# First attention's output turned by transposing SBUF transfers, its projection later in the step

## The chip, the cores and the metric

The kernel runs on one core of one Trainium2 chip. The metric is device time in microseconds of one execution. The engines of the core named here are PE (TensorE, the matrix engine; PEld is its loading of weights), DVE (VectorE), ACT (ScalarE), POOL (GpSimd) and SP (SyncE, which issues transfers here and computes nothing). Each works through its own list of instructions in order; semaphores tie the lists together.

## The reference, cut to what matters

One post-norm decoder layer over 16 sequences of 256 tokens with 256 features: first attention (16 heads of 64, causal), second attention over 77 context rows with a mask, and a mixture of 8 experts (two per token). A normalisation follows each part.

```python
q, k, v = (einsum('bxy,iyk->bxik', x, W).reshape(h, b, t, hs) for W in (Wq, Wk, Wv))
wei = softmax(where(causal, einsum('hbqd,hbkd->hbqk', q, k) * hs ** -0.5, -inf))
out = einsum('hbqk,hbkd->hbqd', wei, v).reshape(b, t, h * hs)
x = layernorm(x + out @ proj_w.T + proj_b)
x = layernorm(x + second_attention(x, ctx, mask))
x = layernorm(x + experts(x))
```

The change concerns the line with `proj_w`: what comes out of first attention has positions on the partitions, and the projection needs it with the features of a head there.

## The kernel before

The program has four parts in a row: both attentions (until about 1010 us), routing, the experts, and a last normalisation. The change is in the first.

The attention part works on 32 tiles of 128 tokens. A step `s` holds work on several tiles at once: q, k and v of tiles `s+1` and `s+2` (`fill`, six pieces a tile, with high and low f16 halves made by ACT, `hi`, and DVE, `lo`), first attention of tile `s` (eight groups: `scores`, DVE's `maxima`, ACT's `exps`, `turn_probs` on PE, high and low halves `pt` by ACT and DVE, `pv` on PE; after each odd group DVE's `normalise`), projection, first norm and most of second attention of tile `s-1` (`stage_c`, pieces 0 to 7), and its end for tile `s-2` (`pv2`, `stage_d`). Nothing is scheduled at run time: in each engine's block a function `step(s)` writes these calls in an order chosen by hand, and the engine runs them in that order. SP's `step` does so for the transfers, all through one queue.

The path that is changed: `normalise` writes the normalised output of two groups into `o_norm`; ACT copies its high half into `o_st` (`o_high`), POOL subtracts for the low half (`split_o`), counted by `s_o_lo`, four a tile. In `stage_c(t, 0)` PE turns `o_st` of the tile by 16 transposes into two PSUM banks, and ACT and DVE each copy one bank into `o_t`. In `stage_c(t, 1)` PE multiplies `o_t` with the projection's weights (32 matmuls into bank c5; in every other step the key and value products of second attention come first), DVE adds the bias to y1, takes statistics (`stats_of`, `moments`), POOL makes the inverse deviation, and DVE's `first_norm` writes x1. `stage_c(t, 2)` begins with PE's transposes of x1. Since `o_norm` has one place, `normalise` waits until POOL has read the pair before.

## Time and profile before

| | us |
|---|---|
| median of 3 runs (lowest, highest) | 1508.05 (1507.47, 1509.12) |
| the profiled execution | 1509.21 |
| its span, first to last instruction | 1507.5 |
| PE busy | 1301.3 (86%) |
| DVE busy | 1083.8 (72%) |
| ACT busy | 924.1 (61%) |
| POOL busy | 721.1 (48%) |
| first and last turn of `o_st` on PE (512 in 32 steps) | 77.9 and 981.5, so 29.1 a step |

A row's busy share is an average over parts with different limits: the attention steps take some 900 of the 1507.5 us, and only there the change does something. Waits are read from a timeline: a row is a run of like instructions, with its start, its time, and in brackets how long the engine had been idle before it and who ended that. Times of PE rows overlap by some 0.15 us, since matmuls are pipelined; the time that a piece takes from PE is that from its start to the next one's.

### The profile page before, as it was taken

To read this page: it belongs to the slowest core of one execution; us is meant where nothing else is said; L and a number is where in the kernel's file an instruction comes from. 1 tells how busy PE (TensorE), PEld (TensorE's weight loads), DVE (VectorE), ACT (ScalarE), POOL (GpSimd) and SP (SyncE) were. 2 spreads that over 40 slices of the span, in tenths; PEclk is the share of its full clock that TensorE was granted. 3 is DMA by queue.
4 is the path that set the end of the run, shared out by engine and by line. 5 is a ranking of instruction groups with operands and counts; after the bars stand their busy time and mean duration, and the time that the engine had idled before them with its cause. 6 is when DMAs were issued, how large, how long until landed. Compare 5 with 4: busy or idle time off the path is not lost. (4 is left out here: it accounts for less than half of the span.)

```text
span 1507.5 us, 47409 instructions
## 1 busy us (share of the span) xinstructions
PE 1301.3 (86%) x16821; PEld 1079.2 (72%) x16821; DVE 1083.8 (72%) x3112; ACT 924.1 (61%) x2287; POOL 721.1 (48%) x970
## 2 busy tenths in 40 slices
PE   3589999999999999999999999864899999999930
PEld 2478778778878877887887887632688888888820
DVE  4678888888888888888888888748455555555537
ACT  3566777778777777777877766514344444444426
POOL 3144564674565566566556644420243344343326
PEclk9899999999999999999999999995899999999975
DMA  9657767667657667676676664019333363333235
GB/s 222 145 138 161 171 169 160 137 145 175 142 140 184 132 140 190 130 150 155 154 154 142 153 105 90 24 61 421 125 75 76 75 163 93 80 75 77 70 139 206
DMA packets 293216, 208.95 MB, mean 139 GB/s; under 512 B 218782, under 2 KB 250654, under 8 KB 290560
## 3 DMA queue, kind: packets, MB, share of 16 engines
q1 hardware_dynamic: 281952, 184.01, 51.0%
q0 software_dynamic: 6816, 17.71, 4.1%
q10 hardware_dynamic: 4224, 4.19, 0.8%
q8 instruction: 146, 2.39, 0.7%
q14 instruction: 78, 0.64, 0.1%
HBM read 93.79 MB, written 65.93 MB: 106 GB/s over the span
## 5 line engine op out<-in xcount | busy, mean ns | idle before, releaser
L1729 PE MATMUL ps_e<-xt,wres 128*128 128x128 f16 x3408 | 343.5, 220 | 5.2 <-DMA xt<-xg 4.2
L1729 PEld LDWEIGHTS ps_e<-xt,wres 128*128 x3408 | 285.8, 99 | 77.1 <-issue 5.9
L1793 ACT ACTIVATE act_g<-ps_e,b 128x128 f32<-128x128 f32 x568 | 162.4, 369 | 208.1 <-PE ps_e L1729 206.3
L1736 PE MATMUL ps_e<-wres,g_hi 128*128 x568 | 214.5, 379 | 0.8 <-DVE g_lo L1816 0.8
L743 ACT ACTIVATE probs<-st_k,nmax 128x128 f32<-128x128 f32 (+1 forms) x512 | 199.9, 448 | 1.9 <-DVE nmax L964 1.6
L964 DVE CUSTOM_DVE_ANT_0 st_k<-ps,causal 128x128 f32<-128x128 f32 (+1 forms) x512 | 160.6, 351 | 38.0 <-PE ps L444 37.9
L1696 POOL DMA_INDIRECT z_scr<-e_y,dst_i x71 | 82.9, 1168 | 212.6 <-DVE e_y L1807 212.6
L750 ACT ACTIVATE pt_hi<-ps 128x384 f16<-128x384 f32 x256 | 125.2, 489 | 56.0 <-PE ps L452 27.7
L1738 PE MATMUL ps_e<-wres,g_lo 128*128 x568 | 154.8, 273 | 0.0
L452 PE MATMUL ps<-ident,probs 128*128 128x128 f32 x768 | 130.5, 279 | 24.4 <-ACT probs L743 19.3
L969 DVE TENSOR_TENSOR pt_lo<-ps,pt_hi 128x384 f16<-128x384 f32 x256 | 141.4, 552 | 6.0 <-ACT pt_hi L750 2.6
L1804 DVE SCALAR_TENSOR_TENSOR e_y<-ps_e,b 128x256 f32<-128x256 f32 x71 | 30.1, 425 | 158.9 <-PE ps_e L1738 158.9
L1271 POOL TENSOR_TENSOR o_st<-o_norm,o_st 128x256 f16<-128x256 f32 x128 | 86.4, 675 | 104.5 <-ACT o_st L758 104.5
L506 PE MATMUL ps<-proj_pair,o_t 128*128 128x256 f16 x1024 | 117.7, 273 | 3.1 <-DVE o_t L1014 3.0
L452 PEld LDWEIGHTS ps<-ident,probs 128*128 128x128 f32 x768 | 86.4, 141 | 45.8 <-ACT probs L743 33.5
L506 PEld LDWEIGHTS ps<-proj_pair,o_t 128*128 128x128 f16 x1024 | 112.2, 146 | 7.2 <-ACT o_t L782 6.8
L1304 POOL TENSOR_TENSOR var_eps<-mv,eps 128x1 f32<-128x1 f32 x64 | 12.3, 192 | 203.1 <-DVE mv L989 203.0
L1392 POOL DMA_INDIRECT xg<-pair_scr,tok_i x71 | 69.7, 982 | 71.7 <-DVE tok_i L1619 42.8
L470 PE MATMUL ps<-v_pos,pt_hi 128*128 128x65 f16 x768 | 90.6, 193 | 13.3 <-DVE o_norm L979 11.2
L422 PE MATMUL ps<-x_hi,w_k 128*128 128x128 f16 x1024 | 97.3, 220 | 0.1
L422 PE MATMUL ps<-x_hi,w_q 128*128 128x128 f16 x1024 | 96.8, 220 | 0.2 <-DVE v_tok L942 0.2
L470 PEld LDWEIGHTS ps<-v_pos,pt_hi 128*128 128x128 f16 x768 | 73.8, 99 | 26.4 <-issue 22.8
(281 smaller groups left out, 4044.9 us busy)
## 6 DMA issues: line engine op xcount, KB each, us to landing
k_pair<-k_pair SPq DMA_DIRECT2D x96, 256.0 KB, 6.6
st_p<-in_moe_w SPq DMA_DIRECT2D x24, 768.0 KB, 5.8
w_scr<-st_p SPq DMA_DIRECT2D x24, 768.0 KB, 4.1
wres<-w_scr SPq DMA_DIRECT2D x18, 1024.0 KB, 20.9
v_scr<-v_tok SPq DMA_DIRECT2D x32, 512.0 KB, 4.2
v_pos<-v_scr SPq DMA_DIRECT2D x64, 256.0 KB, 6.1
q_st<-st_q SPq DMA_DIRECT2D x64, 128.0 KB, 2.8
z_scr<-zero SPq DMA_DIRECT2D x32, 256.0 KB, 3.3
```

Of the source, the lines that this page charges most:

```text
L422: last = mm(bank[:, i * P:(i + 1) * P], w[:, b, c, 4 * n + i].rearrange("p k d -> p (k d)"), xs[a][:, c], start=(m == 0), stop=(m == 5))
L452: last = nc.tensor.transpose(ps_t[:, b * P:(b + 1) * P], probs[:, g % 2, b * P:(b + 1) * P], ident[:])
L470: last = mm(ps_o[:, at:at + 1 + HS], a[:, g % 2, blk * P:(blk + 1) * P], v[:, 0:1 + HS], start=(m == 0), stop=(m == len(todo) - 1), skip_g ...
L506: last = mm(c5[:, 0:D], o_t[:, :, h], wp[:, k, h], start=(h == 0 and k == 0), stop=(h == H - 1 and k == 1))
L743: nc.scalar.activation(probs[:, g % 2, lo_:up_], masked[:, g % 2, lo_:up_], ACT.Exp, bias=nmax[:, g % 2, q:q + 1], scale=-1.0).then_inc(s_ ...
L750: nc.scalar.activation(pt_hi[:, g % 2], ps_t[:, 0:384], ACT.Copy).then_inc(s_pt_hi, 1)
L964: nc.vector.tensor_tensor_reduce(masked[:, g % 2, lo_:up_], ps_s[:, lo_:up_], causal[:].rearrange("p n k -> p (n k)")[:, lo_:up_], -SCORE_ ...
L969: nc.vector.tensor_tensor(pt_lo[:, g % 2], ps_t[:, 0:384], pt_hi[:, g % 2], ALU.subtract).then_inc(s_pt_lo, 1)
L1729: last = mm(out, w(c * FF + f * P, b, P), xt[:, t % X_BUFS, a, c], start=(m == 0), stop=(m == 5))
L1736: mm(out[:, 0:2 * D], g_hi[:, t % G_BUFS, f], w(KC * FF + f * D, 0, 2 * D), start=(f == 0), stop=False, skip_group_check=True)
L1738: last = mm(out[:, 0:D], g_lo[:, t % G_BUFS, f], w(KC * FF + f * D, 0, D), start=False, stop=(f == FC - 1), skip_group_check=True)
L1793: nc.scalar.activation(act_g[:, k % 2, f], ps[:, 3 + 2 * (k % 2) + f // 4, (f % 4) * P:(f % 4 + 1) * P], ACT.Gelu, bias=bias[:, f:f + 1], ...
```

## The change

`o_st` is no longer turned by PE. SP issues transposing transfers from `o_st` to `o_t`, both in SBUF: two for the pairs of groups 1 and 3 together, two for group 5 and two for group 7 (one for each half of the partitions), at the three places of SP's `step` that the diff shows. With that `stage_c(t, 0)` and the two copies into `o_t` are gone, `o_t` has another layout, and the projection reads it so. On PE the projection (`stage_c(s-1, 1)`) is written after `turn_probs(s, 1)` instead of after `scores(s, 3)`; ACT and DVE have their parts of it correspondingly later, and DVE has `lo(s+1, 4)` and the statistics of the second norm ahead of `first_norm`. `o_norm` has two places, so that `normalise` waits for the pair before last. Left out below are the list of semaphores and POOL's two index changes.

```diff
@@ -138,9 +138,9 @@
     rden = sb("rden", [P, 4], F32)
     pt_hi = sb("pt_hi", [P, 2, 384], F16)
     pt_lo = sb("pt_lo", [P, 2, 384], F16)
-    o_norm = sb("o_norm", [P, 4, HS], F32)
+    o_norm = sb("o_norm", [P, 2, 4, HS], F32)
     o_st = sb("o_st", [P, 2, 2 * GROUPS, 2, HS], F16)
-    o_t = sb("o_t", [P, P, H], F16)
+    o_t = sb("o_t", [P, 2, 2 * GROUPS, HS], F16)
     x_bias = sb("x_bias", [P, D], F32)
     y1 = sb("y1", [P, D], F32)
     y2 = sb("y2", [P, D], F32)
@@ -320,6 +320,15 @@
             sp.dma_start(q_st[HS:P, p, :, 1], q_low[HS:P]).then_inc(s_qlow, 16)
             sp.wait_ge(s_qmove, 16 * (t + 1))
             sp.dma_start(q_st[HS:P, p, :, 0], q_low[0:HS]).then_inc(s_qlow, 16)
+
+        def turn_output(t, g):
+            p = t % 2
+            sp.wait_ge(s_o_lo, 4 * t + g // 2 + 1)
+            if g == 3 and since(t, 1):
+                sp.wait_ge(s_proj, t)
+            n = slice(0 if g == 3 else 2 * (g - 1), 2 * (g + 1))
+            for a in range(2):
+                sp.dma_start_transpose(o_t[:, a, n], o_st[a * HS:(a + 1) * HS, p, n].rearrange("p n k d -> p (n k d)")).then_inc(s_ot, 16)
 
         def load_rows(t):
             p = t % 2
@@ -360,6 +369,9 @@
                 load_x(s + 2)
             if has(s + 1):
                 v_out(s + 1)
+            if has(s - 1):
+                turn_output(s - 1, 7)
+            if has(s + 1):
                 v_in(s + 1)
                 key_move(s + 1)
                 key_double(s + 1)
@@ -369,14 +381,19 @@
                 load_context(half(s))
             if has(s + 1):
                 query_move(s + 1)
+            if has(s + 1):
                 query_low(s + 1)
             if has(s - 2):
                 x2_out(s - 2)
                 pair_out(s - 2)
+            if has(s):
+                turn_output(s, 3)
             if 0 <= s - 4 < PIECES:
                 piece_out(s - 4)
             if 0 <= s - 3 < PIECES:
                 piece_in(s - 3)
+            if has(s):
+                turn_output(s, 5)
             if 0 <= s < ZERO_STEPS:
                 zeros(s)
 
@@ -477,18 +494,10 @@
         def stage_c(t, g):
             p = t % 2
             busy(t, BUSY_C.get(g, 0))
-            if g == 0:
-                pe.wait_ge(s_o_lo, 4 * (t + 1))
+            if g == 1:
+                pe.wait_ge(s_ot, 96 * (t + 1))
                 if since(t, 1):
                     pe.wait_ge(s_t2_lo, 4 * t)
-                for half_, bank in enumerate((c5, c6)):
-                    b16 = bank.bitcast(F16)
-                    for n in range(8):
-                        last = nc.tensor.transpose(b16[:, n * P:(n + 1) * P].rearrange("p (t a i) -> p a t i", a=2, i=PAIRS), o_st[:, p, 8 * half_ + n].rearrange("p k d -> p (k d)"), ident16[:])
-                    last.then_inc(s_ot, 1)
-            if g == 1:
-                pe.wait_ge(s_ot_a, t + 1)
-                pe.wait_ge(s_ot_d, t + 1)
                 if t == 0:
                     pe.wait_ge(s_lo, splits_until("xo"))
                 if p == 0:
@@ -503,7 +512,7 @@
                     last.then_inc(s_kv2, 1)
                 for h in range(H):
                     for k in range(2):
-                        last = mm(c5[:, 0:D], o_t[:, :, h], wp[:, k, h], start=(h == 0 and k == 0), stop=(h == H - 1 and k == 1))
+                        last = mm(c5[:, 0:D], o_t[:, h // PAIRS].rearrange("p n (t i) -> p i (n t)", i=PAIRS)[:, h % PAIRS], wp[:, k, h], start=(h == 0 and k == 0), stop=(h == H - 1 and k == 1))
                 last.then_inc(s_proj, 1)
             if g == 2:
                 pe.wait_ge(s_x1, t + 1)
@@ -613,29 +622,26 @@
             if has(s):
                 turn_probs(s, 0)
                 scores(s, 2)
-            if has(s - 1):
-                stage_c(s - 1, 0)
             if has(s - 2):
                 pv2(s - 2, 1)
             if has(s):
                 scores(s, 3)
+                pv(s, 0)
+            if has(s - 2):
+                stage_d(s - 2, 1)
+            if has(s):
+                scores(s, 4)
+                turn_probs(s, 1)
             if has(s - 1):
                 stage_c(s - 1, 1)
-            if has(s):
-                pv(s, 0)
+            if has(s + 1):
+                fill(s + 1, 4)
             if has(s - 1):
                 value_rows(s - 1, 0)
             if has(s - 2):
-                stage_d(s - 2, 1)
-            if has(s):
-                scores(s, 4)
-                turn_probs(s, 1)
+                stage_d(s - 2, 2)
             if has(s - 1):
                 value_rows(s - 1, 1)
-            if has(s + 1):
-                fill(s + 1, 4)
-            if has(s - 2):
-                stage_d(s - 2, 2)
             if has(s):
                 turn_probs(s, 2)
             if has(s - 1):
@@ -754,8 +760,8 @@
             pair = 4 * t + g // 2
             act.wait_ge(s_o_norm, pair + 1)
             if g == 1 and since(t, 2):
-                act.wait_ge(s_ot, 2 * (t - 1))
-            nc.scalar.activation(o_st[:, p, 2 * (g - 1):2 * (g + 1), 0], o_norm[:], ACT.Copy).then_inc(s_o_hi, 1)
+                act.wait_ge(s_ot, 96 * (t - 1))
+            nc.scalar.activation(o_st[:, p, 2 * (g - 1):2 * (g + 1), 0], o_norm[:, pair % 2], ACT.Copy).then_inc(s_o_hi, 1)
 
         def exp2(t, cc):
             act.wait_ge(s_shift, 2 * t + cc + 1)
@@ -777,9 +783,6 @@
 
         def stage_c(t, g):
             p = t % 2
-            if g == 0:
-                act.wait_ge(s_ot, 2 * t + 1)
-                nc.scalar.activation(o_t[:, 0:64].rearrange("p t h -> p (t h)"), c5.bitcast(F16), ACT.Copy).then_inc(s_ot_a, 1)
             if g == 1:
                 if p == 0:
                     act.wait_ge(s_kv2, half(t) + 1)
@@ -828,16 +831,10 @@
                     late_split(0)
             if has(s + 1):
                 hi(s + 1, 3)
-            if has(s - 1):
-                stage_c(s - 1, 0)
             if has(s):
                 exps(s, 2)
-            if has(s - 1):
-                stage_c(s - 1, 1)
             if 0 <= s - 4 < PIECES:
                 piece(s - 4)
-            if has(s - 1):
-                value_rows(s - 1, 0)
             if has(s - 2):
                 stage_d(s - 2, 1)
             if has(s):
@@ -845,9 +842,12 @@
                 if s == 0:
                     late_split(1)
             if has(s - 1):
-                value_rows(s - 1, 1)
+                stage_c(s - 1, 1)
             if has(s + 1):
                 hi(s + 1, 4)
+            if has(s - 1):
+                value_rows(s - 1, 0)
+                value_rows(s - 1, 1)
             if has(s - 1):
                 stage_c(s - 1, 2)
             if has(s):
@@ -974,9 +974,9 @@
             dve.wait_ge(s_pv, 2 * pair + 2)
             nc.vector.reciprocal(rden[:], o[:, :, 0]).then_inc(s_rden, 1)
             dve.wait_ge(s_rden, pair + 1)
-            if since(t, 1) or g > 1:
-                dve.wait_ge(s_o_lo, pair)
-            nc.vector.tensor_tensor(o_norm[:], o[:, :, 1:1 + HS],
+            if since(t, 1) or g > 3:
+                dve.wait_ge(s_o_lo, pair - 1)
+            nc.vector.tensor_tensor(o_norm[:, pair % 2], o[:, :, 1:1 + HS],
                                     rden[:].unsqueeze(2).to_broadcast([P, 4, HS]), ALU.mult).then_inc(s_o_norm, 1)
 
 
@@ -1009,9 +1009,6 @@
 
         def stage_c(t, g):
             p = t % 2
-            if g == 0:
-                dve.wait_ge(s_ot, 2 * t + 2)
-                nc.vector.tensor_copy(o_t[:, 64:128].rearrange("p t h -> p (t h)"), c6.bitcast(F16)).then_inc(s_ot_d, 1)
             if g == 1:
                 if p == 0:
                     dve.wait_ge(s_kv2_hi, 2 * (half(t) + 1))
@@ -1079,10 +1076,6 @@
                 pt(s, 0)
                 if s == 0:
                     late_split(0)
-            if has(s - 1):
-                stage_c(s - 1, 1)
-                stats_of(s - 1, 0, y1, s_y1, s_ln1)
-                moments(s - 1, 0, s_ln1, s_mv1)
             if has(s - 2):
                 stage_d(s - 2, 1)
             if has(s):
@@ -1091,15 +1084,18 @@
                 if s == 0:
                     late_split(1)
             if has(s - 1):
-                first_norm(s - 1)
+                stage_c(s - 1, 1)
+                stats_of(s - 1, 0, y1, s_y1, s_ln1)
+                moments(s - 1, 0, s_ln1, s_mv1)
+            if has(s + 1):
+                lo(s + 1, 4)
             if has(s - 2):
                 stage_d(s - 2, 2)
                 stats_of(s - 2, 1, y2, s_y2, s_ln2)
                 moments(s - 2, 1, s_ln2, s_mv2)
             if has(s - 1):
+                first_norm(s - 1)
                 stage_c(s - 1, 2)
-            if has(s + 1):
-                lo(s + 1, 4)
             if has(s - 2):
                 second_norm(s - 2)
             if has(s):
@@ -1162,8 +1158,6 @@
                 stage_c(s - 1, 7)
             if has(s + 1):
                 maxima(s + 1, 2)
-            if has(s):
-                stage_c(s, 0)
             if has(s + 2):
                 lo(s + 2, 3)
             if has(s - 1):
```

PE's list at the place where the step begins, before the change, in a step without key and value products: `scores(s, 3)` (k_pair), the projection (o_t), and the first row of `pv(s, 0)` (v_pos).

```order
L441 MATMUL ps<-k_pair,q_st 128x128 [waits s1_11_max]
L442 MATMUL ps<-k_pair,q_st 128x128
L443 MATMUL ps<-k_pair,q_st 128x256
L444 MATMUL ps<-k_pair,q_st 128x256
L506 MATMUL ps<-proj_pair,o_t 128x256 [waits s1_23_ot_d,s1_22_ot_a]
L506 MATMUL ps<-proj_pair,o_t 128x256 x31
L470 MATMUL ps<-v_pos,pt_hi 128x65 [waits s1_18_o_norm,s1_9_v_in,s1_15_pt_lo]
```

The same place after the change.

```order
L458 MATMUL ps<-k_pair,q_st 128x128 [waits s1_11_max]
L459 MATMUL ps<-k_pair,q_st 128x128
L460 MATMUL ps<-k_pair,q_st 128x256
L461 MATMUL ps<-k_pair,q_st 128x256
L487 MATMUL ps<-v_pos,pt_hi 128x65 [waits s1_18_o_norm,s1_9_v_in,s1_15_pt_lo]
L490 MATMUL ps<-v_pos,pt_hi 128x64
```

The rows of `pv(s, 0)`, which wait for DVE's low halves of the probabilities (pt_lo), now follow the scores directly. The projection stands behind the transposes of probabilities of group 1 and before the fill of q, as PE's list after the change shows:

```order
L469 MATMUL ps<-ident,probs 128x128 [waits s1_15_pt_lo,s1_12_exp]
L469 MATMUL ps<-ident,probs 128x128 x2
L515 MATMUL ps<-proj_pair,o_t 128x256 [waits s1_46_t2_lo,s1_21_ot]
L515 MATMUL ps<-proj_pair,o_t 128x256 x31
L439 MATMUL ps<-x_hi,w_q 128x128 [waits s1_7_fill_lo]
```

It waits for `s_ot`, which the transfers now raise.

DVE's list from y1 to the first norm (the row `x<-y,mv,rstd`) before the change:

```order
L1026 SCALAR_TENSOR_TENSOR y<-ps,x_bias 128x256 [waits s1_xb,s1_24_proj]
L985 BN_STATS stats<-y 128x6 [waits s1_25_y1]
L989 BN_AGGR mv<-stats 128x2 [waits s1_26_ln1]
L1059 TENSOR_TENSOR o_lo<-ps,o_hi 128x256 [waits s1_53_o2_hi]
L964 ISA st_k,nmax<-ps,causal 128x128 [waits s1_12_exp,s1_10_scores]
L964 ISA nmax 128x1
L964 ISA st_k,nmax<-ps,causal 128x256
L964 ISA nmax 128x1
L969 TENSOR_TENSOR pt_lo<-ps,pt_hi 128x384 [waits s1_14_pt_hi]
L1008 TENSOR_SCALAR x<-y,mv,rstd 128x256 [waits s1_27_rstd1]
```

And after it:

```order
L969 TENSOR_TENSOR pt_lo<-ps,pt_hi 128x384 [waits s1_14_pt_hi]
L1023 SCALAR_TENSOR_TENSOR y<-ps,x_bias 128x256 [waits s1_xb,s1_22_proj]
L985 BN_STATS stats<-y 128x6 [waits s1_23_y1]
L989 BN_AGGR mv<-stats 128x2 [waits s1_24_ln1]
L950 TENSOR_TENSOR st_q<-ps,q_st 128x128x4 [waits s1_qlow,s1_6_fill_hi]
L1060 SCALAR_TENSOR_TENSOR y<-ps,x 128x256 [waits s1_53_proj2]
L985 BN_STATS stats<-y 128x6 [waits s1_54_y2]
L989 BN_AGGR mv<-stats 128x2 [waits s1_55_ln2]
L1008 TENSOR_SCALAR x<-y,mv,rstd 128x256 [waits s1_25_rstd1]
```

The maxima and pt_lo of group 1 have moved ahead of y1; the low half of q (st_q, which waits for ACT's high half of that fill) and y2 with its statistics now stand between y1's moments and the norm.

SP's list around the end of a step, after the change (before it, the four DMA_TRANSPOSE rows are missing):

```order
L331 DMA_TRANSPOSE o_t<-o_st 128x8x64 [waits s1_22_proj,s1_20_o_lo]
L331 DMA_TRANSPOSE o_t<-o_st 128x8x64
L280 DMA w_scr<-st_p 128x3072 [waits s1_w_lo]
L276 DMA st_p<-in_moe_w 128x1536 [waits s1_w_lo]
L331 DMA_TRANSPOSE o_t<-o_st 128x4x64 [waits s1_20_o_lo]
L331 DMA_TRANSPOSE o_t<-o_st 128x4x64
L257 DMA x_t<-in_xT 128x2x128 [waits s1_4_x_lo]
L289 DMA v_scr<-v_tok 128x2x1024 [waits s1_9_v_in,s1_7_fill_lo,s1_6_fill_hi]
```

The third pair of transposes, for group 7, follows that last row (`v_out`) and stands before `v_in`. So `load_x` and `v_out` are queued behind the transposes of group 5, and `v_in` behind those of group 7.

## Rows read from the trace of the kernel before

**Rows 1.** Busy time by stage: stage, its us, each engine's busy us, PE clock, DMA share, GB/s
```profile
300.00:500.00 200.00, 188.19 (x2630) 163.07 (x2627) 169.58 (x550) 155.14 (x337) 118.77 (x169) 1.00 0.67 155
```

**Rows 2.** PE's timeline, one step from scores(s, 2): start, us, instructions, idle before
```profile
574.88 0.22 PE L441 MATMUL ps<-k_pair,q_st 128*128 128x128 f16 x1
...
575.22 1.06 PE L487 MATMUL ps<-ident,o_st 128*128 128x128 f16 x16
576.11 0.18 PE L577 MATMUL ps<-st_xq,pt_hi 128*128 128x34 f16 x1
...
576.49 0.22 PE L441 MATMUL ps<-k_pair,q_st 128*128 128x128 f16 x1
...
577.15 3.69 PE L506 MATMUL ps<-proj_pair,o_t 128*128 128x256 f16 x32 [0.16 <-DVE o_t L1014]
580.67 0.19 PE L470 MATMUL ps<-v_pos,pt_hi 128*128 128x65 f16 x1
...
581.86 0.22 PE L422 MATMUL ps<-x_hi,w_q 128*128 128x128 f16 x1
...
583.20 0.27 PE L597 MATMUL ps<-xw_o,o_hi 128*128 128x256 f16 x1
...
584.18 0.38 PE L513 MATMUL ps<-ident,x 128*128 128x128 f32 x2
...
587.24 0.49 PE L452 MATMUL ps<-ident,probs 128*128 128x128 f32 x3
```

**Rows 3.** DVE's timeline in the same step
```profile
576.31 0.69 DVE L1014 COPY o_t<-ps 128x1024 f16<-128x1024 f16 x1 [0.25 <-PE ps L487]
576.92 0.68 DVE L953 SCALAR_TENSOR_TENSOR k_pair<-ps,k_pair 128x512 f16<-128x512 f32 x1
...
578.14 0.28 DVE L964 CUSTOM_DVE_ANT_0 st_k<-ps,causal 128x128 f32<-128x128 f32 x1
...
578.69 0.55 DVE L969 TENSOR_TENSOR pt_lo<-ps,pt_hi 128x384 f16<-128x384 f32 x1
580.88 0.42 DVE L1026 SCALAR_TENSOR_TENSOR y<-ps,x_bias 128x256 f32<-128x256 f32 x1 [1.63 <-PE ps L506]
...
581.89 0.39 DVE L1059 TENSOR_TENSOR o_lo<-ps,o_hi 128x256 f16<-128x256 f32 x1
...
583.22 0.41 DVE L1008 TENSOR_SCALAR x<-y,mv,rstd 128x256 f32<-128x256 f32 x1
```

**Rows 4.** PE's timeline in step 0: scores(0, 3) and pv(0, 0)
```profile
51.62 0.23 PE L441 MATMUL ps<-k_pair,q_st 128*128 128x128 f16 x1 [0.74 <-DVE nmax L964]
...
54.28 0.20 PE L470 MATMUL ps<-v_pos,pt_hi 128*128 128x65 f16 x1 [2.16 <-DVE pt_lo L969]
```

**Rows 5.** ACT's timeline in the step of rows 2: the high half of q
```profile
583.39 0.60 ACT L732 ACTIVATE q_st<-ps 128x512 f16<-128x512 f32 x1 [0.85 <-PE ps L422]
```

**Rows 6.** PE's timeline later in that step, and in the next
```profile
600.93 0.77 PE L545 MATMUL ps<-ident,probs 128*128 128x128 f32 x5 [0.70 <-ACT probs L767]
...
623.84 0.19 PE L470 MATMUL ps<-v_pos,pt_hi 128*128 128x65 f16 x1 [0.56 <-DVE o_norm L979]
```

**Rows 7.** The tile xt of the experts: ns min/median/max, first and last start in us
```profile
L1729 PE MATMUL ps_e<-xt,wres x3408: 219/219/314, 1068.1 to 1441.6; 128*128 128x128 f16 x190
L1769 SPq DMA_TRANSPOSE xt<-xg x71: 1189/1190/2646, 1065.2 to 1427.5; - x71
```

**Rows 8.** DMA queues, 1250 to 1400 us: packets, MB, share of 16 engines
```profile
q1 hardware_dynamic: 15776, 3.80, 14.2%
```

**Rows 9.** POOL's (o_st) and SP's timelines around the start of the step of rows 2
```profile
571.77 0.67 POOL L1271 TENSOR_TENSOR o_st<-o_norm,o_st 128x256 f16<-128x256 f32 x1
574.40 0.67 POOL L1271 TENSOR_TENSOR o_st<-o_norm,o_st 128x256 f16<-128x256 f32 x1 [1.96 <-ACT o_st L758]
...
570.18 0.93 SPq L257 DMA_DIRECT2D x_t<-in_xT  x1
573.21 0.38 SPq L289 DMA_DIRECT2D v_scr<-v_tok  x1
```

More of the change, by code:

```diff
@@ L198, in attention_block @@
     (s_xt, s_xn, s_ctx, s_x_hi, s_x_lo, s_fill, s_fill_hi, s_fill_lo, s_v_out, s_v_in, s_scores, s_max,
-     s_exp, s_pt, s_pt_hi, s_pt_lo, s_pv, s_rden, s_o_norm, s_o_hi, s_o_lo, s_ot, s_ot_a, s_ot_d, s_proj, s_y1,
+     s_exp, s_pt, s_pt_hi, s_pt_lo, s_pv, s_rden, s_o_norm, s_o_hi, s_o_lo, s_ot, s_proj, s_y1,
      s_ln1, s_rstd1, s_x1, s_x1t, s_x1_hi, s_x1_lo, s_c_hi, s_c_lo, s_q2, s_q2_hi, s_q2_lo, s_kv2, s_kv2_hi,
@@ L204, in attention_block @@
         "xt xn ctx x_hi x_lo fill fill_hi fill_lo v_out v_in scores max exp pt pt_hi pt_lo pv rden o_norm o_hi "
-        "o_lo ot ot_a ot_d proj y1 ln1 rstd1 x1 x1t x1_hi x1_lo c_hi c_lo q2 q2_hi q2_lo kv2 kv2_hi kv2_lo bd s2 "
+        "o_lo ot proj y1 ln1 rstd1 x1 x1t x1_hi x1_lo c_hi c_lo q2 q2_hi q2_lo kv2 kv2_hi kv2_lo bd s2 "
         "pred mx2 shift exp2 t2 t2_hi t2_lo pv2 rden2 o2n o2t o2_hi o2_lo proj2 y2 ln2 rstd2 x2 x2_hi x2_lo "
@@ L633, in step @@
             if has(s - 1):
-                value_rows(s - 1, 1)
+                stage_c(s - 1, 1)
             if has(s + 1):
                 fill(s + 1, 4)
+            if has(s - 1):
+                value_rows(s - 1, 0)
             if has(s - 2):
                 stage_d(s - 2, 2)
+            if has(s - 1):
+                value_rows(s - 1, 1)
             if has(s):
@@ L830, in step @@
                 hi(s + 1, 3)
-            if has(s - 1):
-                stage_c(s - 1, 0)
             if has(s):
                 exps(s, 2)
-            if has(s - 1):
-                stage_c(s - 1, 1)
             if 0 <= s - 4 < PIECES:
                 piece(s - 4)
-            if has(s - 1):
-                value_rows(s - 1, 0)
             if has(s - 2):
@@ L847, in step @@
             if has(s - 1):
-                value_rows(s - 1, 1)
+                stage_c(s - 1, 1)
             if has(s + 1):
                 hi(s + 1, 4)
+            if has(s - 1):
+                value_rows(s - 1, 0)
+                value_rows(s - 1, 1)
             if has(s - 1):
@@ L1081, in step @@
                     late_split(0)
-            if has(s - 1):
-                stage_c(s - 1, 1)
-                stats_of(s - 1, 0, y1, s_y1, s_ln1)
-                moments(s - 1, 0, s_ln1, s_mv1)
             if has(s - 2):
@@ L1093, in step @@
             if has(s - 1):
-                first_norm(s - 1)
+                stage_c(s - 1, 1)
+                stats_of(s - 1, 0, y1, s_y1, s_ln1)
+                moments(s - 1, 0, s_ln1, s_mv1)
+            if has(s + 1):
+                lo(s + 1, 4)
             if has(s - 2):
@@ L1270, in split_o @@
             pool.wait_ge(s_o_hi, pair + 1)
-            nc.gpsimd.tensor_tensor(at[:, :, 1], o_norm[:], at[:, :, 0], ALU.subtract).then_inc(s_o_lo, 1)
+            nc.gpsimd.tensor_tensor(at[:, :, 1], o_norm[:, pair % 2], at[:, :, 0], ALU.subtract).then_inc(s_o_lo, 1)
         def split_x2(t):
```

## Prediction

> **What bounds the kernel now.** I read the table of stages first: where the attention steps run (300 to 500 us), PE is busy 188.19 of 200 us at a granted clock of 1.00, DVE 169.58, ACT 155.14, and the DMA engines 0.67 [rows 1]. PE is the bound, with about 6% idle: with the table's 29.1 us a step that is 29.1 x 11.81/200 = 1.7 us of waits a step. DVE comes close behind and, since every engine runs its list in order, what decides is not the sum of PE's work but which of its waits are covered. So I read PE's timeline through one step, from `scores(s, 2)` at 574.88 on [rows 2], and beside it DVE's for the same stretch [rows 3]. The reader should see two things. PE has almost no holes: 16 transposes, the rest of second attention's value product, scores, then 32 projection matmuls from 577.15 to 580.67. And DVE, at 578.14, is only then doing the maxima of `scores(s, 3)` and at 578.69 the low halves of the probabilities of group 0, which PE's `pv(s, 0)` waits for. PE comes to `pv(s, 0)` at 580.67, when they have been ready since 578.69 + 0.55 = 579.24. The projection is what PE does meanwhile; DVE then has nothing to do for 1.63 us until the projection lands [rows 3].
>
> **What is removed.** Per step: the 16 transposes, 576.11 - 575.22 = 0.89 us of PE; the hole before the projection, of which 0.16 us is a wait for DVE's copy and which is 0.33 us in all (577.15 - 576.49 = 0.66, less 0.33 for the four score matmuls, 574.88 to 575.22) [rows 2]. On DVE the copy (0.69 us), on ACT its twin. If nothing else changed PE would gain 0.89 + 0.33 = 1.22 us a step.
>
> **What is moved: the first wait.** In the new order PE goes from `scores(s, 2)` through pv2 (0.38) and `scores(s, 3)` (0.33) straight to `pv(s, 0)`, which it reaches 0.34 + 0.38 + 0.33 = 1.05 us after 574.88, at 575.93, if nothing holds it. DVE's order before that probability block is unchanged but for the copy: maxima 2 (done at 576.31 - 0.25 = 576.06, the copy's row says that DVE was idle 0.25 us before it), then the low half of k, the reciprocal and the normalised second output (576.92 to 578.14, 1.22 us), maxima 3 (0.55), pt_lo (0.55): 576.06 + 2.32 = 578.38 [rows 3], 578.44 with a handover. PE thus waits 578.44 - 575.93 = 2.5 us, part of it before `scores(s, 3)` (which needs maxima 2), most before `pv(s, 0)`. The trace of before shows this very order once: step 0 has no projection to put there, and PE waited 0.74 us before `scores(0, 3)` and 2.16 us before `pv(0, 0)`, 2.9 us together [rows 4]. Bounds: 2.0 (if half the DVE chain were done earlier) and 2.9; I take 2.5.
>
> **The second wait.** The projection itself keeps its 3.52 us (577.15 to 580.67). What lies between `pv(s, 0)` and it costs 581.86 - 580.67 = 1.19 as before, so it starts at 578.44 + 1.19 = 579.63 and ends at 583.15. Behind it, PE now has only the fill (581.86 to 583.20, 1.34) and the output product of second attention with a turn of probabilities (583.20 to 584.18, 0.98) before it transposes x1: it wants x1 at 585.47. DVE's way to x1: y1 starts 0.21 after PE has moved on, its sum, statistics and moments take 581.89 - 580.88 = 1.01. But three things now stand ahead of the norm on DVE: `lo(s+1, 4)`, which must wait for that fill and ACT's high half (ACT ends 583.39 + 0.60 = 583.99 where PE's fill ended 583.20, so 0.79 later [rows 5]: 584.49 + 0.79 = 585.28), takes about 0.7; then y2 with its statistics, another 1.01; then the norm, 0.41 [rows 3]. 585.28 + 0.06 for the handover + 0.7 + 1.01 + 0.41 = 587.5. PE waits 2.0 us for x1, where before x1 was there at 583.22 + 0.41 = 583.63 and PE came at 584.18. POOL's two small operations fall into DVE's wait. Bounds: 0 if DVE's list were not in order, 2.1.
>
> From x1's transposes to the turn of group 3 nothing changes (584.18 to 587.24, 3.06), so that turn stands at 587.5 + 3.06 = 590.56: 3.32 us later in the step than before (2.5 + 2.0 - 1.2, less rounding).
>
> **What is given back.** After that point PE's old waits can absorb some. Two are shown: 0.70 us before second attention's transposes (for ACT's exponentials, behind a long POOL chain) and, in every other step, 0.56 us before a pv, for a normalised output that stood behind POOL's subtraction [rows 6]. The second goes away with two places of `o_norm`. The first is at the end of a chain that starts at the shifted softmax scores, which are themselves about 3 us late; I count 0.27 back (bounds 0 and 0.70). Two steps: 2 x 3.32 - 0.27 - 0.56 = 5.8 us. Steps 1 to 31 hold 15.5 such pairs: **+90 us**. All of PE's idle, 1.7 us a step, would be the most that could be absorbed: 31 x (3.32 - 1.7) = +50 us, the lower bound.
>
> **The transposing transfers.** The trace has 71 of the kind, 128 x 512 f16 (128 KB) each: 1.19 us of SP's queue (slowest 2.65), first issue at 1065.2 and first matmul on its result at 1068.1, so landed within 2.9 us [rows 7]. In a stretch with 29 of them queue 1 held 16 engines 14.2% of 150 us, 0.73 us each [rows 8]. A step moves 512 KB in six issues, so 4 x 0.73 = 2.9 us of the engines in 32: no new bound beside 0.67. When is the last pair there? POOL ends pair 2 at 571.77 + 0.67 = 572.44. SP then issues two transposes (0.6 each by bytes, 1.19 by instruction), `load_x` (0.93), `v_out` (0.38), then the last two, whose data POOL had at 575.07 [rows 9]: the second of these is issued at 575.7 to 577.4 and lands by 578.6 to 580.3. PE wants it at 579.63. Late by 0 to 0.7; I take 0.25, nearer the issue by bytes: 31 x 0.25 = **+8 us**. With the slowest issue of the trace each time (2.65) it would be 5 us late. The other queued transfers (v, k and q moves) shift by 2 to 3 us with `v_out`; their readers stand near the end of the step. The drained last step pays a transfer's latency where 0.89 us of transposes and a copy stood: +1 us.
>
> The row says 0.73 us of engine time for four blocks of 128 x 128. The Trainium skill (VectorE: DVE Perf Modes, "The three transpose paths") gives 1309 ns for one such block by DMA against 390 ns by TensorE, and advises TensorE when PSUM will do. By its figure taken block by block, an estimate, the last four blocks would take 5.2 us in place of 2.9, some 2 us later a step; I keep the row.
>
> **Sum.** 1509.21 us, the profiled execution (span 1507.5), + 90 + 8 + 1 = 1608. The median of the runs shown is 1.2 us below that execution: **1607 us**, slower by 6.5%.
>
> **Rivals.**
> - *Late transposes.* Issue cost goes by instruction, or halves of 64 partitions cost more than 128, and PE waits for o_t 2 us or more a step. For it: six issues stand in one in-order queue with transfers that wait for each other. Against: rows 7 and 8. 1599 + 31 x 2 = 1661, from 1645 up.
> - *Mostly absorbed.* PE's own 1.7 us of waits vanish, since DVE and ACT have 0.69 and 1.0 us less to do: 1508 + 50 + up to 8 = 1558 to 1566. Against: the waits listed are tails of chains that the projection starts.
> - *Faster.* PE is the bound and sheds 1.22 us a step: 1508 - 31 x 1.22 = 1470. It decides if DVE has pt_lo of group 0 within 0.7 us of `scores(s, 2)` and x1 within 2.3 us of the projection; the rows give 3.2 and 4.35. It would need DVE to be ahead of PE, and DVE waits for PE there (maxima 2 start 0.2 us after the scores).
> - *No change.* The two cancel by chance.
>
> **Numbers.** Forecast (1575 to 1645) 0.64, late transposes 0.13, absorbed (1530 to 1575) 0.13, faster 0.07, no change 0.03. The range 1553 to 1662 holds the forecast, most of the absorbed and half of the late case, 0.8. About 0.2% is what a measurement of this kernel tells from no change: slower 0.90, same 0.03, faster 0.07.
>
> **What will show it.** In the changed trace: PE waits near 2 us before the first `pv` of each step, released by DVE's pt_lo, and near 2 us before the x1 transposes, released by DVE's norm; a pair of steps takes 58 + 6 us; the row of o_t transposes shows how SP pays, and PE's wait before the projection whether they land in time. If the first two waits are under 1 us the forecast is wrong; if the wait before the projection is the largest, the second case holds.

## The result and the profile after

The changed kernel takes **1751.91 us** (median of 4 runs, 1748.35 to 1756.93) against 1508.05 of the kernel before: ratio 1.162, 95% interval 1.158 to 1.165. It is slower, as forecast, but by 244 us and not by 99; the range ended at 1662. Of the rivals the late transposes came closest, and they too were priced too low (1661). By the prediction's own sign that case holds: of PE's waits between 200 and 900 us the one for the transfers is the largest (56.4 us, against 42.8 before `scores(s, 3)` and `pv(s, 0)` and 25.6 for x1).

The table of stages of the changed kernel, same columns and stretch as [rows 1]:

```profile
300.00:500.00 200.00, 157.17 (x1999) 129.25 (x1996) 135.25 (x440) 120.31 (x270) 98.38 (x137) 0.92 0.63 133
```

PE is busy 157 of 200 us, not 188, and its granted clock is 0.92 where it was 1.00. The second number is the one nobody had asked for. The first projection starts at 92.1, the last at 1233.0: 36.8 us a step against 29.1, so 7.7 us more. Where they go, PE's timeline of one step shows (start, us, what, idle before and who ended it; to be held against [rows 2]):

```profile
571.61 0.22 PE L458 MATMUL ps<-k_pair,q_st 128*128 128x128 f16 x1
...
572.84 0.23 PE L458 MATMUL ps<-k_pair,q_st 128*128 128x128 f16 x1 [0.37 <-DVE nmax L964]
...
575.21 0.20 PE L487 MATMUL ps<-v_pos,pt_hi 128*128 128x65 f16 x1 [1.87 <-DVE pt_lo L969]
...
576.08 0.49 PE L469 MATMUL ps<-ident,probs 128*128 128x128 f32 x3
579.83 5.75 PE L515 MATMUL ps<-proj_pair,o_t 128*128 128x256 f16 x32 [3.26 <-DMA o_t<-o_st]
585.42 0.22 PE L439 MATMUL ps<-x_hi,w_q 128*128 128x128 f16 x1
...
589.64 0.44 PE L522 MATMUL ps<-ident,x 128*128 128x128 f32 x2 [1.74 <-DVE x L1008]
```

Both forecast waits are there: 0.37 + 1.87 us around `scores(s, 3)` and `pv(s, 0)` (forecast 2.5) and 1.74 us before the x1 transposes (forecast 2.0). Two things are not as forecast. The projection waits 3.26 us for the transposing transfers (forecast 0.25), and it then lasts from 579.83 to 585.42, 5.59 us in place of 3.52, which the forecast had left alone. The table of stages, cut along that stretch, says why; the last three columns are PE's granted clock, the DMA share and GB/s:

```profile
575.21:576.57 1.36, 1.36 (x18) 1.10 (x18) 0.00 (x0) 0.00 (x0) 0.00 (x0) 1.00 1.02 343
576.57:579.83 3.26, 0.00 (x0) 0.00 (x1) 0.00 (x0) 3.00 (x3) 0.00 (x0) 0.61 0.88 251
579.83:582.00 2.17, 2.17 (x11) 1.70 (x12) 1.44 (x6) 0.62 (x2) 0.00 (x0) 0.50 0.65 107
582.00:585.42 3.42, 3.42 (x24) 2.94 (x23) 0.00 (x0) 0.00 (x0) 0.00 (x0) 0.69 1.41 117
585.42:587.90 2.48, 2.48 (x35) 2.19 (x32) 1.35 (x4) 0.60 (x1) 0.76 (x2) 1.00 0.80 174
```

The clock fell to half (0.50: 1.2 in place of 2.4 GHz) while PE stood idle, and the projection began at that level: 11 matmuls in 2.17 us. The next stretch has 0.69 in the mean; in it the clock came back to 1.00, at about 584.1, when 4.2 us of the projection were over. Over the whole run the projection's group shows it too; before, the mean of one matmul was 273 ns and the sum 117.7 us, and `pv` had waited 13.3 us in all where its line now has 61.9:

```profile
L515 PE MATMUL ps<-proj_pair,o_t 128*128 128x256 f16 x1024 | 165.1, 338 | 54.7 <-DMA o_t<-o_st 54.7
L487 PE MATMUL ps<-v_pos,pt_hi 128*128 128x65 f16 x768 | 91.8, 194 | 61.9 <-DVE pt_lo L969 60.5
```

Why the transfers are late is read on POOL's and SP's own timelines of that step; the first two rows are POOL's low halves for groups 5 and 7, the rest is SP's queue, where a row's time is what the issues occupy SP (before: [rows 9]):

```profile
568.50 0.67 POOL L1265 TENSOR_TENSOR o_st<-o_norm,o_st 128x256 f16<-128x256 f32 x1
571.12 0.67 POOL L1265 TENSOR_TENSOR o_st<-o_norm,o_st 128x256 f16<-128x256 f32 x1 [1.96 <-ACT o_st L764]
...
566.70 2.55 SPq L331 DMA_TRANSPOSE o_t<-o_st  x2
569.29 1.54 SPq L280 DMA_DIRECT2D w_scr<-st_p  x1
570.88 0.43 SPq L276 DMA_DIRECT2D st_p<-in_moe_w  x1
571.36 3.16 SPq L331 DMA_TRANSPOSE o_t<-o_st  x2
574.57 0.59 SPq L257 DMA_DIRECT2D x_t<-in_xT  x1
575.26 0.43 SPq L289 DMA_DIRECT2D v_scr<-v_tok  x1
575.74 2.60 SPq L331 DMA_TRANSPOSE o_t<-o_st  x2
```

From 566.70 to 578.34 SP has no pause. Group 5's data are ready at 569.17 and are issued from 571.36 on; group 7's are ready at 571.79 and issued from 575.74 on. A pair costs 2.55 us where its halves are 128 KB (the pairs of groups 1 and 3) and 2.60 where they are 64 KB (group 7): SP pays by instruction. The row of the tile `o_t` gives the same over 192 issues (ns, lowest, median, highest), with the time that PE lost before the projection (L515) or, in the steps with key and value products, before those (L508), and how long a transfer took to land:

```profile
L331 SPq DMA_TRANSPOSE o_t<-o_st x192: 1170/1266/2811, 74.3 to 1224.3; - x192
...
  PE ps L515: 54.7, 15
...
  PE ps L508: 35.6, 14
...
DMA to landing us min/median/max: 2.3/3.7/7.4
```

So PE lost 54.7 + 35.6 = 90.3 us to the transfers in the whole run.

### The profile page after: what moved, and what is told of

It is laid out like the page before. It is cut to its first block and busy times, and to the rows that moved or that the text cites. A ratio compares the mean times of both kernels' runs of the same rounds, so it can differ in the third digit from the quotient of the medians.

```text
span 1755.1 us, 46505 instructions
## 1 busy us (share of the span) xinstructions
PE 1351.8 (77%) x16306; PEld 1087.7 (62%) x16306; DVE 1074.4 (61%) x3080; ACT 895.2 (51%) x2255; POOL 724.2 (41%) x970
## 3 DMA queue, kind: packets, MB, share of 16 engines
q10 hardware_dynamic: 4224, 4.19, 0.7%
## 5 line engine op out<-in xcount | busy, mean ns | idle before, releaser
L515 PE MATMUL ps<-proj_pair,o_t 128*128 128x256 f16 x1024 | 165.1, 338 | 54.7 <-DMA o_t<-o_st 54.7
L515 PEld LDWEIGHTS ps<-proj_pair,o_t 128*128 128x128 f16 x1024 | 139.4, 154 | 80.7 <-DMA o_t<-o_st 58.9
L469 PE MATMUL ps<-ident,probs 128*128 128x128 f32 x768 | 135.3, 286 | 28.3 <-ACT probs L749 23.7
L738 ACT ACTIVATE q_st<-ps 128x512 f16<-128x512 f32 x64 | 38.2, 597 | 203.6 <-PE ps L439 203.6
L487 PE MATMUL ps<-v_pos,pt_hi 128*128 128x65 f16 x768 | 91.8, 194 | 61.9 <-DVE pt_lo L969 60.5
L1284 POOL TENSOR_TENSOR k_bd<-head_rows,k 128x308 f16<-128x308 f16 x64 | 45.3, 728 | 169.5 <-DVE v L1019 169.5
L1386 POOL DMA_INDIRECT xg<-pair_scr,tok_i x71 | 69.6, 980 | 73.5 <-DVE tok_i L1613 42.8
## 6 DMA issues: line engine op xcount, KB each, us to landing
wres<-w_scr SPq DMA_DIRECT2D x18, 1024.0 KB, 23.2
```

The costliest lines, as they stand in the source:

```text
L469: last = nc.tensor.transpose(ps_t[:, b * P:(b + 1) * P], probs[:, g % 2, b * P:(b + 1) * P], ident[:])
L487: last = mm(ps_o[:, at:at + 1 + HS], a[:, g % 2, blk * P:(blk + 1) * P], v[:, 0:1 + HS], start=(m == 0), stop=(m == len(todo) - 1), skip_g ...
L515: last = mm(c5[:, 0:D], o_t[:, h // PAIRS].rearrange("p n (t i) -> p i (n t)", i=PAIRS)[:, h % PAIRS], wp[:, k, h], start=(h == 0 and k == ...
```

## Experiments

Three theories of the missing 145 us. **A, the order**: the waits for DVE are larger than forecast, or others joined them. **B, SP's queue**: the transfers are late because of where they stand among SP's issues. **C, the clock**: PE runs slower behind its new waits. All times are medians; each set was timed beside the kernel before (1508.2 to 1508.5).

### The order alone

```diff
             if g == 1:
-                pe.wait_ge(s_ot, 96 * (t + 1))
+                pe.wait_ge(s_ot_a, t + 1)
+                pe.wait_ge(s_ot_d, t + 1)
...
                 scores(s, 2)
+            if has(s - 1):
+                stage_c(s - 1, 0)
```

> The changed kernel's order on every engine and its two places for the normalised output, but the kernel before's turning: 16 TensorE transposes a step and the two copies out of PSUM, no transposing transfer. The order alone. By the forecast the order costs 90 us net of the transposes and the hole that went, 1.22 us x 32 = 39 us; with the transposes back, 0.89 x 32 = 28: 1508 + 90 + 28 = 1626, range 1600 to 1650. If the lower clock behind the new waits comes with the order and not with the transfers, 1650 to 1690. If the order is harmless and the transfers are all of the loss: 1500 to 1540.

Measured 1661.05, ratio 1.101 (1.098 to 1.104). The order costs 153 us without any transfer, 35 more than the 118 that the waits of the forecast give (1508 + 90 + 28 = 1626). Its waits between 200 and 900 us (total, times, longest):

```profile
PE ps L472 <- DVE pt_lo L969: 48.7, 21, 2.3
PE ps L515 <- DVE x L1008: 26.5, 20, 1.7
```

They are 2.3 and 1.3 us a step, no more than forecast. The wait for x1 is 1.74 and 0.91 us in turn: the larger one, near the forecast 2.0, in the steps without key and value products, the kind that the forecast read, the smaller one in the others. But the clock is 0.96 between 300 and 500 us here, and a projection matmul takes 296 ns. In one step PE stood for 2.32 us, until 322.81, waiting for pt_lo, and from 323 to 326 us, in which the projection began, the granted clock was 0.50.

### The order alone, PE kept working

```diff
                 scores(s, 3)
+                idle_work(s, 8)
                 pv(s, 0)
```

`idle_work` are matmuls of 512 columns on constants, into a bank that is written anew before it is read.

> The run of the order alone (TensorE transposes and copies, the changed order) with 8 matmuls of 512 columns, on operands that are there and into a bank that nobody reads, ahead of pv(s,0), where TensorE waits 2.3 us a step for pt_lo. The order alone measured 1661 where the waits of the forecast give 1626. If the 35 us are the lower clock behind that wait, the time falls by 25 to 40, to 1620 to 1636. If they are other waits: 1655 to 1670.

Measured **1620.18**, 41 us less, with more work on PE. The wait for pt_lo is down to 12.5 us, the other is as it was, and the clock is 1.00 again:

```profile
300.00:500.00 200.00, 177.57 (x2357) 147.31 (x2355) 153.11 (x490) 136.18 (x302) 107.70 (x152) 1.00 0.60 135
...
PE ps L521 <- DVE x L1015: 27.4, 21, 1.7
...
PE ps L478 <- DVE pt_lo L976: 12.5, 21, 0.6
```

C holds for the order: 41 us of its 153 go with the clock. What is left, 112, is the 118 of the forecast within 6: A is ruled out as the miss, though the 6 come of two errors that nearly cancel (below).

### The changed kernel, PE kept working

```diff
                 scores(s, 3)
+                idle_work(s, 8)
                 pv(s, 0)
...
+                idle_work(s, 11)
                 stage_c(s - 1, 1)
```

> The changed kernel with matmuls put into two of its waits, on operands that are there and into a bank that nobody reads: 8 of 512 columns ahead of pv(s,0), 11 ahead of the projection (some 0.22 us each at full clock, 1.8 and 2.4 us, less than the two waits of 1.9 and 3.3 us). They change nothing but what TensorE does while it waits. If the lower clock after these waits costs time by itself (theory: the projection takes 5.6 us in place of 3.5 because the clock is at half in it), the projection comes back to about 3.5 us and the time falls by 45 to 65 us, to 1687 to 1707. If the clock is low for another reason, or the time that the projection loses is waited for elsewhere anyway, 1740 to 1765. If the matmuls stand before work that is ready: up to 1780.

Measured 1718.91, 33 us less than the changed kernel: in the direction of C, and less than its 45 to 65. PE's clock is 0.99 between 300 and 500 us, and the projection's group is down from 165.1 to 128.4 us, 37 us, about what the kernel gained:

```profile
L521 PE MATMUL ps<-proj_pair,o_t 128*128 128x256 f16 x1024 | 128.4, 288 | 29.7 <-DMA o_t<-o_st 29.7
```

At 288 ns a matmul, not 273, the projection is not wholly at the upper level; PE still waits for the transfers behind the 11 matmuls, 29.7 us before the projection alone.

### Without the last pair of transfers

```diff
-            if has(s - 1):
-                turn_output(s - 1, 7)
...
-                pe.wait_ge(s_ot, 96 * (t + 1))
+                pe.wait_ge(s_ot, 64 * (t + 1))
...
+        nc.vector.memset(o_t[:, :, 12:16], 0.0).then_inc(s_one, 1)
```

> The changed kernel without group 7's transposing transfers: the last quarter of the turned output is a constant zero, so a quarter of the projection's input is left out. The transfers of groups 3 and 5 have landed long before the projection. If the transfers' lateness is what was sized wrongly and the rest stands as forecast (order and waits for DVE: about +90 us over the kernel before), the wait for the turned output goes to 0 and the time to 1590 to 1650, the lower half if the clock stays up too. If the order itself was sized wrongly: 1680 or more with no wait for the turned output left.

Measured 1643.02: 109 us are tied to group 7's pair. PE's wait for transfers is down to 6.7 us in the whole run, from 90.3. The clock is still low (0.93 between 300 and 500 us, with the wait for pt_lo as it was), which fits a time at the upper end.

### The six transfers in a row, ahead of the weight piece

```diff
             if has(s):
                 turn_output(s, 3)
+                turn_output(s, 5)
+                turn_output(s, 7)
             if 0 <= s - 4 < PIECES:
                 piece_out(s - 4)
```

> The changed kernel with the same six transposing transfers, in one row on SP's queue: group 7's directly behind group 5's, in the same step, ahead of the piece of the expert weights, the load of x and v_out (SP alone is reordered, and ScalarE's two weight pieces go behind pt(s,1), since their load now comes later). If the transfers are late because of where they stand on SP, where each instruction takes about 1.27 us, group 7's pair begins near 572 in place of 575.74 in the step that was read, the projection's wait falls from 3.3 to under 1 us, and the time falls by 70 to 100 us, to 1650 to 1680, some 45 more if the clock then stays up (1605 to 1635). If the transfers are late because they take so long in the DMA engines: 1735 to 1760. If the loads that now stand behind them become the wait: over 1700 with new DMA rows on TensorE or ScalarE.

Measured 1750.57: nothing gained. Read by its time alone this would refuse B. Its waits between 200 and 900 us say otherwise:

```profile
PE ps L520 <- DVE x L1006: 47.3, 18, 5.1
...
PE ps L568 <- DVE v L1017: 19.2, 9, 2.8
PE ps L456 <- issue: 13.0, 12, 6.2
...
PE ps L513 <- DMA o_t<-o_st: 0.2, 1, 0.2
```

The wait for the transfers is gone (0.2 us), and a wait for x1 of up to 5.1 us stands in its place, with two others. The cause of the first is on ACT's timeline:

```profile
571.42 1.48 ACT L821 ACTIVATE st_p<-st_p 128x1536 f16<-128x1536 f32 x1 [3.94 <-DMA st_p<-in_moe_w]
572.93 1.48 ACT L823 ACTIVATE st_p<-st_p 128x1536 f32<-128x1536 f32 x1
574.32 0.58 ACT L736 ACTIVATE q_st<-ps 128x512 f16<-128x512 f32 x1
```

The load of the weight piece now stands behind six transposes. ACT waits 3.94 us for it, and q's high half is queued behind; DVE's `lo(s+1, 4)`, y2 and the norm wait for that half. The run was confounded by its own edit, and the next one mends it.

### The six transfers in a row, behind the weight piece

```diff
                 piece_in(s - 3)
             if has(s):
+                turn_output(s, 3)
                 turn_output(s, 5)
+                turn_output(s, 7)
```

> The changed kernel with the six transposing transfers in one row on SP's queue, as in the run that put group 7 behind group 5, but behind the piece of the expert weights, not ahead of it, and ScalarE's order as in the changed kernel: the weight piece that ScalarE waits for is then issued some 3 us earlier than in the changed kernel, and no new wait is made. Group 7's pair begins when the other four are through, about 573.2 to 573.5 in the step that was read, 2.3 to 2.5 us earlier than 575.74. If the place on SP is what makes the turned output late, the projection's wait falls from 3.3 to about 1 us a step, the time by 60 to 80 us and some 20 to 40 more if the clock stays up: 1640 to 1690. If the reordering moves the loss to another wait again, as it did with the weight piece: 1730 to 1755.

Measured **1650.86** (1646.57 and 1655.15): 101 us less by the order of SP's list alone, the same six transfers and the same bytes, which take as long from issue to landing (median 3.6 us, 3.7 in the changed kernel). PE's wait for the transfers is 8.1 us in the whole run (from 90.3), 7.7 of it before the projection:

```profile
  PE ps L513: 7.7, 8
```

B holds. With its place on SP mended the change is 10 us under the order alone (1661), where 0.25 us of lateness and 0.89 us of saved transposes had promised 8 - 28 = -20. The traces show where the rest went. From the fifth projection on (232.92 to 1125.78 us, against 222.19 to 1135.96) the kernel is 21 us faster than the order alone; until then it is 11 us slower. In the first steps PE waits 5.25, 4.83 and 4.19 us before `scores` with no releaser named; this wait is 23.2 us in the whole run and was 10.3 in the changed kernel. SP's list has the writes of zeros in the first four steps as well; which transfer is late there was not tested.

### Both at once

```diff
                 scores(s, 3)
+                idle_work(s, 8)
                 pv(s, 0)
```

on the kernel of the section before.

> The run with the six transposing transfers in a row behind the weight piece (1651), with the 8 matmuls on unread data ahead of pv(s,0) that took 41 us off the order alone. If the two things that the forecast of 1607 left out are SP's place for the transfers and the clock behind TensorE's wait for pt_lo, and nothing else, this kernel gives about the forecast: 1651 - 41 = 1610, range 1595 to 1625. If the two overlap, or a third loss is there: 1635 or more.

Measured 1629.10, 22 us less and not 41, 4 us above the expected range and 22 above the forecast of 1607. The clock is 1.00; PE is earlier, and the transfers, which keep their time, are late again by about 0.5 us a step, 14.9 us in all with 2.0 before the key and value products:

```profile
  PE ps L519: 12.9, 14
```

So the two losses overlap in part: this wait is 7 us more than in the run before and than forecast. The first steps are the other part of what is left over the forecast: the fifth projection starts at 227.97, where the order alone with PE kept working has 216.06, 12 us earlier. 7 + 12 is about the 22. This is read from the traces and was not tested; the gain of 22 in place of 41 is accounted for in part only, by the 7.

### The second wait undone

```diff
                 moments(s - 1, 0, s_ln1, s_mv1)
+                first_norm(s - 1)
             if has(s + 1):
                 lo(s + 1, 4)
...
-                first_norm(s - 1)
                 stage_c(s - 1, 2)
```

on the order alone with PE kept working (1620).

> The order alone with the 8 matmuls ahead of pv(s,0) (1620), with VectorE's first_norm put directly behind the moments of y1, ahead of lo(s+1,4) and the statistics of y2: the second wait of the forecast undone. If x1 is late because of what VectorE does ahead of it, it can come at POOL's 1/deviation, 0.9 to 1.5 us earlier a step; TensorE's wait for x (1.3 us a step) falls under 0.5, the time by 25 to 40 us, to 1580 to 1595. If the wait for x is that chain itself, whatever stands in it, or lo(s+1,4) and y2 are then late in its place: 1610 to 1625.

Measured 1603.07, 17 us less, between the two ranges. The wait for x1 is gone (2.6 us between 200 and 900 us, from 27.4), and with a wait of 1.3 us a step it should have given 40 us. Part of it has come back in waits that were smaller (L553: 10.4 us) or not there:

```profile
PE ps L553 <- ACT probs L775: 15.8, 22, 0.7
...
PE ps L545 <- DVE q_lo L1041: 4.9, 22, 0.3
PE ps L521 <- ACT st_xv L784: 3.6, 11, 0.3
...
PE ps L521 <- DVE x L1015: 2.6, 11, 0.2
```

So what DVE does ahead of the norm is what made x1 late, as forecast, but taking that away gives back less than half of what it costs: this wait lost 25 us between 200 and 900 us, and the first three rows have gained 14. Why those grew was not tested.

### Transposing transfers in the order of before

Two mixtures were meant as faster kernels. They keep the order of before and two places of `o_norm`. In the first SP turns groups 1, 3 and 5, PE the last 4 blocks; in the second SP turns groups 1 and 3, PE 8 blocks. DVE alone copies. The first mixture:

```diff
             if has(s):
+                turn_output(s, 3)
+                turn_output(s, 5)
...
-                    for n in range(8):
+                for n in range(4):
```

> The kernel before's order, with two places for the normalised output; groups 1, 3 and 5 of the output are turned by four transposing transfers, which SP issues behind the weight piece, and TensorE turns the last 4 of 16 blocks only, with one VectorE copy of 128x512 (ScalarE's copy goes). If the transfers are in time where the projection comes at 577.2 (group 5's are issued near 572.7 to 575.3 and land up to 3.7 us later by the median): 12 of 16 transposes saved, 0.67 us a step, and part of the 0.16 to 0.43 us that the projection waits for the copies: 1475 to 1492. If group 5's land after 577.2: each us late costs 32 us, 1500 to 1560.

> The same with groups 1 and 3 alone turned by two transposing transfers; TensorE turns 8 blocks into one bank and VectorE copies them (0.69 us, as now), ScalarE's copy goes. Group 3's transfers have some 4 us to spare: 8 transposes saved, 0.45 us a step or 14 us, 1485 to 1497. If SP's queue, longer by 2.5 us a step, makes x, v or the keys late: 1508 or more.

Measured 1557.61 (ratio 1.032, 1.030 to 1.034) and 1519.42 (1.008, 1.006 to 1.010): both slower than before. The projection, earlier in the step here, waits for the transfers; PE's waits of the first mixture and of the second between 200 and 900 us:

```profile
PE ps L517 <- DMA o_t<-o_st: 28.9, 11, 4.0
...
PE ps L510 <- DMA o_t<-o_st: 6.8, 9, 2.4
```

```profile
PE ps L516 <- DMA o_t<-o_st: 15.8, 9, 2.7
```

In the whole run they are 39.0 and 16.8 us. In the first, SP's four issues behind the weight piece take 7.10 us in the step that was read, 1.8 each, and the projection's matmuls take 134.5 us in all, 117.7 before, at a clock of 0.97 between 300 and 500 us. A last run puts the second mixture's pair ahead of the weight piece:

```diff
+            if has(s):
+                turn_output(s, 3)
             if 0 <= s - 4 < PIECES:
                 piece_out(s - 4)
```

> The kernel before's order with 8 of 16 blocks turned by two transposing transfers (1519), with these two ahead of the weight piece on SP's queue, and POOL's subtraction for group 3 ahead of the last third of its own weight piece. If they land late only because the piece, 768 KB, is ahead of them in the queues, the projection's wait for them (35 us in the trace) goes, and the saved 8 transposes are left: 1484 to 1497, faster than the kernel before. If the piece then makes ScalarE late, or SP's longer queue the loads: 1505 to 1530.

(The 35 us named there are idle time of PE and of its weight loads added up; PE's own wait is the 16.8 us.) Measured 1529.52 (1.014, 1.012 to 1.016), 10 us more. The projection's wait for transfers is gone from its list of waits, and another, 2.7 us before, has come between 200 and 900 us:

```profile
PE ps L452 <- issue: 25.5, 11, 3.9
```

L452 is the first matmul of `scores`, which waits for moved keys and queries; "issue" means that the trace names nobody who released it. That SP's longer queue makes these moves late fits, but was not shown.

### Two places of `o_norm` alone

```diff
-    o_norm = sb("o_norm", [P, 4, HS], F32)
+    o_norm = sb("o_norm", [P, 2, 4, HS], F32)
```

on the kernel before.

> The kernel before with two places for the normalised output and nothing else. TensorE waits there for o_norm 6.7 us in 700, 12 times, in one step of two; if that is all that the second place takes away, 0.2 to 0.3 us a step, 1500 to 1505. If what the wait holds up waits for something else anyway: 1507 to 1510.

Measured 1507.37, ratio 0.9991 (0.9982 to 1.0000): no difference that can be told. PE's waits for o_norm (6.7 us between 200 and 900 us) are gone, and the wait before second attention's transposes has grown from 8.3 to 16.9 us there: what the wait held up waits for the exponentials anyway.

## Why the prediction was wrong

- **Removed, 1.22 us a step.** Right for the transposes: behind the first four steps the kernel with the six transfers in a row gains 21 us on the order alone, as 28 us of transposes less 8 of waits would have it. The hole of 0.33 us was not tested by itself.
- **First wait, 2.5 us.** Right: 2.24 us in the step that was read, 2.3 with the order alone.
- **Second wait, 2.0 us.** Right in its place and cause, too large in size: 1.74 in the step that was read, 0.91 in the steps with key and value products, 1.3 in the mean. The forecast put one kind of step for both, some 0.7 us x 31 = 21 us too much.
- **+90 us for the order.** Right without the clock, 1620 measured against 1626 by the same terms, but in part by luck. Against the 21 us too much stand the 0.27 + 0.56 us in two steps (13 us) that PE's old waits were to give back and did not: in the order alone with PE kept working, PE's other waits are 33.8 us in some 21 steps between 200 and 900 us, and all its waits were 34.8 in some 24 steps before.
- **Not in the sum: the clock.** The step "the projection itself keeps its 3.52 us" failed. The two waits ahead of it were counted as idle time only; they also bring PE's clock to half, and the work behind them takes longer. That cost 41 us with the order alone, and 33 in the changed kernel as far as filling the waits could show it. [rows 1] gives the clock as 1.00 for a PE with 6% of holes; what it would be behind longer ones was not asked.
- **The transfers, +8 us.** This is the larger failure. PE's side was right: it wanted the output 4.75 us after `scores(s, 2)` by the forecast, 4.96 in the trace (571.61 to 576.57). The output was to land 3.7 to 5.4 us after it and came after 8.2. The step that failed is "SP then issues two transposes": it let SP begin with group 5 when POOL had its data, as if SP were free, and left out group 3's pair and the weight piece, which the list of SP shows right ahead of it; and it took an issue as 0.6 us, nearer the price by bytes, where it is 1.27 by instruction. The second was the upper bound, and was named; the first was not in the bounds at all. In the step that was read SP came to group 5's pair 2.19 us after its data, and this pair took 3.16 us where the upper bound had 2.38; together about the 2.9 us by which group 7's second issue, counted from group 5's data, is later than by the upper bound. What it cost is the 91 us between the order alone and the changed kernel. An estimate from the two traces comes to the same: 90.3 us of waits, less 28 of transposes, and 165.1 - 134.1 = 31 us more for the projection's matmuls, some of them at the lower clock, give 93. The order of SP's list takes 101 us off again, with the price of an issue as it was (median 1.25 us): at that price the place alone mends it.
- **The late rival.** Its two reasons, issue by instruction and one queue in order, were the right ones; the order of the queue is the one that a run tested, and issue by instruction was not enough by itself, since the upper bound had it. "Against: rows 7 and 8" was no evidence: [rows 7] had given 1.19 us for an instruction, and [rows 8] spoke of the DMA engines, which were not the limit, since the same transfers in another order of SP's list are nearly in time.

The Trainium skill (VectorE: DVE Perf Modes, "Rules for kernel authors") advises TensorE for a 128 x 128 transpose where PSUM will do. No run here with transposing transfers beat the kernel before, so the advice held. Its price per block is not what decided: the transfers were late by their place in SP's queue, as one run with another order of the same transfers shows.

In sum, as steps from run to run: 1508 + 112 (order) + 41 (clock behind it) + 91 (transfers in SP's queue, their share of the clock with them) = 1752. In another order of the steps the shares differ, since the losses overlap: 101 for the place on SP first, then 22 for the clock.

## What to carry to other kernels

Before work is moved to transfers, write down the issuing engine's whole list around the place, with each issue at the price that the trace shows for one instruction, and let it start when the instruction ahead ends, not when its data are ready. Where an order takes the cover off a wait on a PE that had none, price the lower clock behind it as well as the wait; a table of stages with the granted clock shows it at once. And an experiment that changes nothing in time may still have removed what it aimed at: read its waits before the theory is dropped. Waits are read on the engine itself: the idle time that a tile's view gives adds up PE and its weight loads (113.6 us in the changed kernel, where PE lost 90.3).

## What the runs showed of the hardware

- A transposing transfer within SBUF occupied SP's queue for 1.27 us (median of 192), with 128 KB no more than with 64 KB (pairs of 2.55 and 2.60 us in the step that was read), and up to 2.81. The 71 transposing transfers of the experts had given 1.19 [rows 7].
- PE idle for 1.87 us, 1.36 us of work, then idle for 3.26 us: in that last stretch the granted clock fell from 1.00 to 0.50, and 11 projection matmuls took 2.17 us where 20 would have gone at 0.11 each. Matmuls on unread data in these stretches kept the clock at 0.99 to 1.00 and made the kernel 33 and 41 us faster with more work. The Trainium skill (TensorE: Matmul & The Clock Gate, "HAM oscillation — how this bites in real kernels") tells of a loop whose waits for transfers bring the clock down each time round; the trace agrees, and with the order alone a wait for another engine did it as well: 2.32 us for pt_lo, then 0.50 from 323 to 326 us, and 1.00 in the mean once that wait was filled.
